# Gating matmuls behind the softmax normalisation in all four head quartets of an attention and FFN kernel, instead of the last one

## The chip, the cores and the metric

One Trainium2 chip with 8 NeuronCores. The batch of 32 sequences is split evenly, 4 sequences for each core, and every core runs the same program; there is no traffic between cores. The metric is the device time of one execution on the slowest core, in microseconds (us). TensorE is called PE here, ScalarE ACT, VectorE DVE, GpSimd POOL and SyncE SP.

## The reference

One pre-norm transformer layer on x of shape (32, 2048, 1024), in float32:

```
x = x + attention(layernorm(x))      # 16 heads of 64, additive mask, softmax over keys
x = x + ffn(layernorm(x))            # 1024 -> 64 -> (64x16 relu) -> 64 -> 1024

qkv    = encodings @ attn_w.T + attn_b
mask   = arange(n)[:, None] <= arange(n)[None, :]          # key <= query
scores = where(mask, einsum('bhki,bhqi->bhkq', k, q) / sqrt(64), -10000)
probs  = softmax(scores, axis=2)
out    = einsum('bhkq,bhkl->bhql', probs, v) -> @ out_w.T + out_b
```

## The kernel before

**Stages.** A core walks 16 stages: for each of its 4 sequences the four query blocks g = 0 to 3 of 512 queries. A stage is `attention(sq, g)`, then the output projection, second layernorm and FFN of its four 128-row tiles (`epilogueA`, `epilogueB`), interleaved with the layernorm, transposes and the Q, K and V projections of the next stage (`phaseA_ln`, `phaseA_tr`, `phaseA_qkv`).

**Order.** The program text is the order on each engine: each helper call appends one operation to the list of its engine, with the semaphore values that it must wait for. An engine runs its list in order; nothing passes a waiting instruction on the same engine. `deps` is what the operation waits for.

**Attention.** Query block g needs the key tiles kt = 0 to 4(g+1)-1 of 128 keys, so 4, 8, 12 or 16 of them. The 16 heads are handled as four quartets u = 0 to 3, each of two head pairs pi = 0 and 1. For each key tile and pair there are two score matmuls (L352, L356: the two heads of the pair, each contracting 64 rows in its own half of the array) into the 1024 float32 columns of P0 that belong to the pair, one exponential on ACT over both heads (L361) into `s_probs`, and, for the last four key tiles alone (the diagonal), a mask multiplication on DVE (L369). The value matmuls (L389, four for each key tile: two pairs by two heads) are emitted one key tile behind: scores of kt, then values of kt-1. They accumulate into P1 (pair 0) and P2 (pair 1); row 64 of each carries the softmax sum, because V has a column of ones.

**Normalisation.** Behind the last value matmul of a quartet, for each pair in turn: Ln of the sums (L404, on one partition by 1024), Exp of minus that (L407), a DMA of the 4 KB row to DRAM from ACT's queue (d1, L409), a DMA from POOL's queue that reads it back onto 64 partitions (d2, L411), and two DVE multiplications that write `s_comb` (L421) and so free the pair's P1 or P2. The first value matmuls of the next quartet wait for these multiplications (`pv_done`), since they overwrite the same banks. The scores of the next quartet wait for the exponentials that last read P0, and for nothing of the normalisation.

**The gating matmuls.** In the last quartet (u = 3) each pair's normalisation is followed on PE by three matmuls of 128x128 by 128 columns (L430), of the identity by itself, into columns 1536 to 1663 of P0. Nobody reads their result. The first waits for the pair's Ln, the second for its Exp, the third for the arrival of d2. Behind them on PE stands the output projection of `epilogueA`.

Of the kernel before, what the change touches and what calls it, by code (L numbers as in the profile page):

```python
# [95 lines left out]
def build_program(nseq=NSEQ):  # L96
# [20 lines left out]
    with ExitStack() as st:  # L117
# [11 lines left out]
        s_id = e(nc.sbuf_tensor("s_id", [128, 128], BF16))  # L129
# [14 lines left out]
        P0 = e(nc.psum_tensor("P0", [128, 2048], F32))  # L144
# [3 lines left out]
        s = Sched(nc)  # L148
# [181 lines left out]
        def attention(sq, g):  # L330
# [6 lines left out]
            for u in range(4):  # L337
# [3 lines left out]
                for kt in range(nkt + 1):  # L341
                    newpend = None
                    if kt < nkt:
# [4 lines left out]
                        for pi, hp in enumerate(pairs):  # L348
# [6 lines left out]
                                start=True, stop=True), deps=deps_sc)  # L355
# [3 lines left out]
                                start=True, stop=True), deps=[])  # L359
# [5 lines left out]
                                deps=[t_s1, st_["probs_pv"][pi * 2 + kt % 2]])  # L365
# [11 lines left out]
                    if pending is not None:  # L377
# [3 lines left out]
                        for pi, hp in enumerate(pairs):  # L381
                            for hi in range(2):
# [10 lines left out]
                                    start=f, stop=l, skip_group_check=True),  # L393
                                    deps=[pdeps[pi]] + dep_f)
                            st_["probs_pv"][pi * 2 + pkt % 2] = t_last_pv[pi]
                    pending = newpend
                for pi, hp in enumerate(pairs):
                    t_lp = t_last_pv[pi]
                    Ppv = P1 if pi == 0 else P2
                    zc = st_["zchain"] % 4  # L400
                    st_["zchain"] += 1
                    zrow = (s_zz[32:33, 0:1024] if pi == 0
                            else s_zz[96:97, 0:1024])
                    tln = s.op("act", lambda E, P=Ppv, zr=zrow: E.activation(  # L404
                        zr, P[64:65, 0:1024], AF.Ln),
                        deps=[t_lp, st_["zr_read"][pi], st_["zz_read"][pi]])
                    tex = s.op("act", lambda E, zr=zrow: E.activation(  # L407
                        zr, zr, AF.Exp, scale=-1.0), deps=[tln])
                    d1 = s.dma("act", f"ch_z{zc}", zscr.ap()[zc:zc + 1, :], zrow,  # L409
                               deps=[tex, st_["zscr_read"][zc]])  # L410
                    d2 = s.dma("pool", f"ch_zb{zc}", s_zz[pi * 64:(pi + 1) * 64, :],  # L411
                               bass.AP(zscr, zc * 1024, [[0, 64], [1, 1024]]),
                               deps=[d1, st_["zz_read"][pi]])
                    st_["zr_read"][pi] = d1
                    st_["zscr_read"][zc] = d2
                    for hi in range(2):
                        bank = 2 * pi + hi
                        hh = 2 * hp + hi
                        pvX = pv_banks[bank]
                        zb = s_zz[pi * 64:(pi + 1) * 64, hi * 512:(hi + 1) * 512]  # L420
                        tcm = s.op("dve", lambda E, P=pvX, c=hp, hh2=hh, z=zb: E.tensor_tensor(  # L421
                            s_comb[(hh2 % 2) * 64:(hh2 % 2) * 64 + 64, c * QB:(c + 1) * QB],
                            P[0:64, 0:512], z, ALU.mult),
                            deps=[d2, st_["comb_read"]])
                        st_["pv_done"][bank] = tcm
                        comb_written.append(tcm)
                    st_["zz_read"][pi] = comb_written[-1]
                    if u == 3:
                        for wdep in (tln, tex, d2):
                            s.op("pe", lambda E: E.matmul(  # L430
                                P0[:, 1536:1664], s_id[:, :], s_id[:, :],
                                start=True, stop=True), deps=[wdep])
            st_["P1_freed"] = comb_written[-1]
            st_["P2_freed"] = comb_written[-1]
            return comb_written
# [132 lines left out]
        phaseA_qkv(*stages[0])  # L568
        for idx, (sq, g) in enumerate(stages):
            comb = attention(sq, g)  # L570
            nxt = stages[idx + 1] if idx + 1 < len(stages) else None
            slot = lambda i: (idx * GT + i) % 6
# [109 lines left out]
```

How the kernel before makes its waits and increments, by code:

```python
            def run(engine):  # L80
                for emit, waits, inc_sem, inc in oplist:
                    for (sname, val) in waits:
                        engine.wait_ge(sems[sname], val)
                    ins = emit(engine)
                    if ins is not None and inc_sem is not None:
                        ins.then_inc(sems[inc_sem], inc)
```

## Time and profile before

| | us |
|---|---|
| time before, median of 2 runs (4315.42 to 4316.69) | 4316.06 |
| the profiled execution's own time | 4316.25 |
| its span, slowest core | 4314.3 |
| spans of the 8 cores | 4296.1 to 4314.3 |
| mean granted PE clock of the cores | 0.759 to 0.764 |
| PE busy | 2790.8 (65%) |
| PE weight loads busy | 1077.9 (25%) |
| ACT busy | 1803.0 (42%) |
| DVE busy | 1110.3 (26%) |

A busy share is an average over stages of different kinds. The granted clock is a share of full speed: 1.0 is 2.4 GHz and 0.5 is 1.2 GHz. In rows of the trace, "idle before" is the time that the engine stood still ahead of an instruction, with what released it; a row "x2" merges two instructions that follow each other.

### The profile page before, as it was taken

How to read it: one execution, taken by the hardware profiler on the slowest of the kernel's cores; microseconds unless marked ns; L12 is line 12 of the kernel's file. 1: busy time of each engine (PE TensorE's matmuls, PEld its weight loads, DVE VectorE, ACT ScalarE, POOL GpSimd, SP SyncE). 2: the span in 40 equal slices, each digit the busy share in tenths (PEclk: the TensorE clock that was granted, in tenths of full speed). 3: DMA queues.
4: the chain of work that ended last, by engine and by line, in shares of the span. 5: the costliest groups of instructions: out<-in, count | busy, mean ns of one | idle time of the engine just before them, and what ended most of it. 6: DMA issues, size and time to landing. Idle time of an engine off the chain costs nothing.

```text
span 4314.3 us, 40073 instructions; the slowest of 8 cores (4296.1 to 4314.3 us)
## 1 busy us (share of the span) xinstructions
PE 2790.8 (65%) x12384; PEld 1077.9 (25%) x12384; DVE 1110.3 (26%) x2486; ACT 1803.0 (42%) x2945; POOL 100.3 (2%) x196
## 2 busy tenths in 40 slices
PE   0657676686656658677674756757666576765874
PEld 0222232232222223232231312223222132322322
DVE  3141311402323141230323223031131413214112
ACT  0424337166141625517523251643733234272481
POOL 0000000000000000000000000000000000000000
PEclk9868787698676768768776776878877677776886
DMA  6010000100101000010000001000000000000000
GB/s 199 15 35 20 26 24 20 40 6 15 39 20 39 15 35 15 15 39 10 20 30 30 30 20 39 11 20 30 15 25 28 32 25 25 30 15 30 10 10 25
DMA packets 36934, 122.00 MB, mean 28 GB/s; under 512 B 7610, under 2 KB 7738, under 8 KB 36732
## 3 DMA queue, kind: packets, MB, share of 16 engines
q0 software_dynamic: 19456, 67.12, 4.4%
q1 hardware_dynamic: 17020, 51.80, 3.9%
q8 instruction: 110, 1.80, 0.2%
q14 instruction: 92, 0.75, 0.1%
q10 hardware_dynamic: 256, 0.52, 0.0%
HBM read 85.34 MB, written 34.08 MB: 28 GB/s over the span
## 4 chain that ended last, share of the span: by engine, by line
PE 48%; ACT 17%; DVE 11%; issue 11%; DMA 10%; ACTq 1%; DVEq 0%; SPq 0%; POOLq 0%
PE P L314 10%; PE P L389 10%; ACT s_probs L361 7%; PE P L291 6%; PE P L449 6%; DMA s_zz<-zscr 5%; PE P L352 5%; DMA zscr<-s_zz 3%; ACT s_zz L407 3%; ACT s_zz L404 3%; DVE s_xln L219 2%; DVE s_probs L492 2%; DVE s_x L460 2%; PE P L544 2%; PE P L548 2%
## 5 line engine op out<-in xcount | busy, mean ns | idle before, releaser
L361 ACT ACTIVATE s_probs<-P 128x1024 bf16<-128x1024 f32 (+3 forms) x1280 | 1062.8, 894 | 403.2 <-PE P L356 248.9
L389 PE MATMUL P<-s_probs,s_vaug 128*65 128x512 bf16 (+3 forms) x2560 | 721.7, 398 | 199.3 <-DVE s_comb L421 109.6
L352 PE MATMUL P<-s_q,s_k 64*128 64x512 bf16 (+3 forms) x1280 | 466.3, 392 | 429.4 <-ACT s_probs L361 395.0
L369 DVE TENSOR_TENSOR s_probs<-s_probs,s_tril 128x256 bf16<-128x256 bf16 x512 | 145.7, 292 | 1401.0 <-ACT s_probs L361 1398.6
L356 PE MATMUL P<-s_q,s_k 64*128 64x512 bf16 (+3 forms) x1280 | 475.3, 399 | 0.0
L314 PE MATMUL P<-s_xlnT,s_wqk 128*128 128x512 bf16 x2048 | 444.8, 379 | 0.0
L389 PEld LDWEIGHTS P<-s_probs,s_vaug 128*65 128x65 bf16 x2560 | 247.3, 119 | 568.1 <-issue 473.3
L449 PE MATMUL P<-s_ow,s_comb 128*128 128x512 bf16 x1024 | 331.4, 482 | 39.6 <-DVE s_x L552 39.6
L237 ACT ACTIVATE s_stats<-s_stats 128x1 f32<-128x1 f32 x128 | 37.7, 294 | 752.1 <-DVE s_stats L234 752.1
L421 DVE TENSOR_TENSOR s_comb<-P,s_zz 64x512 bf16<-64x512 f32 x256 | 175.0, 683 | 671.6 <-DMA s_zz<-zscr 667.6
L481 PE MATMUL P<-s_id,s_xln 128*128 128x128 bf16 x512 | 107.8, 258 | 370.4 <-ACT s_probs L488 276.2
L352 PEld LDWEIGHTS P<-s_q,s_k 64*128 64x128 bf16 x1280 | 108.9, 95 | 817.3 <-issue 811.4
L323 ACT ACTIVATE s_q<-P,s_bqk 128x512 bf16<-128x512 f32 x128 | 88.0, 688 | 449.8 <-PE P L314 449.8
L291 PE MATMUL P<-s_wv,s_xlnT 128*128 128x512 bf16 x1024 | 266.8, 408 | 8.3 <-ACT s_xlnT L276 8.3
L314 PEld LDWEIGHTS P<-s_xlnT,s_wqk 128*128 128x128 bf16 x2048 | 199.1, 98 | 241.5 <-issue 3.6
L276 ACT CAST s_xlnT<-P 128x128 bf16<-128x128 f32 x512 | 98.9, 274 | 181.8 <-PE P L270 181.0
L404 ACT ACTIVATE s_zz<-P 1x1024 f32<-1x1024 f32 x128 | 130.1, 1016 | 78.3 <-PE P L389 37.2
L449 PEld LDWEIGHTS P<-s_ow,s_comb 128*128 128x128 bf16 x1024 | 108.6, 115 | 216.6 <-issue 165.5
L219 DVE SCALAR_TENSOR_TENSOR s_xln<-s_x 128x1024 bf16<-128x1024 f32 x128 | 156.3, 1221 | 12.3 <-DMA s_x<-x 5.2
L481 PEld LDWEIGHTS P<-s_id,s_xln 128*128 128x128 bf16 x512 | 50.2, 105 | 425.2 <-issue 419.4
L300 DVE CAST s_vaug<-P 128x512 bf16<-128x512 f32 x128 | 88.8, 694 | 248.7 <-PE P L295 245.0
L270 PE MATMUL P<-s_id,s_xln 128*128 128x128 bf16 x512 | 76.8, 265 | 108.5 <-DVE s_xln L246 105.0
(60 smaller groups left out, 2028.4 us busy)
## 6 DMA issues: line engine op xcount, KB each, us to landing
s_x<-x SPq DMA_DIRECT2D x64, 512.0 KB, 4.0
s_zz<-zscr POOLq DMA_DIRECT2D x128, 256.0 KB, 3.5
out<-s_x POOLq DMA_DIRECT2D x64, 512.0 KB, 2.9
s_x<-wqk_t SPq DMA_DIRECT2D x16, 512.0 KB, 7.3
s_x<-wv_t SPq DMA_DIRECT2D x8, 512.0 KB, 6.2
s_x<-ow_t SPq DMA_DIRECT2D x8, 512.0 KB, 6.2
zscr<-s_zz ACTq DMA_DIRECT2D x128, 4.0 KB
s_x<-bias_rows SPq DMA_DIRECT2D x1, 260.0 KB
```

Source lines behind the costliest of these rows:

```text
L219: tsq = s.op("dve", lambda E: E.scalar_tensor_tensor(dst_xln[:, :], src[:, :], 1.0, src[:, :], ALU.mult, ALU.mult, accum_out=s_stats[:, cQ ...
L291: s.op("pe", lambda E, cc=c, ii=i, rr=r, p=pacc: E.matmul(p, s_xlnT[:, cc * QB + ii * 128: cc * QB + (ii + 1) * 128], s_wv[:, cc * 1024 + ...
L314: tmm = s.op("pe", lambda E, f=fc, cc=c, p=pacc: E.matmul(p, s_wqk[:, cc * 2048 + f * 128: cc * 2048 + (f + 1) * 128], s_xlnT[:, cc * QB:( ...
L352: s.op("pe", lambda E, c=hp, k=kt, c0=col0, S=SC: E.matmul(S[:, c0:512], s_k[0:64, c * T + k * 128: c * T + (k + 1) * 128], s_q[0:64, c * ...
L356: t_s1 = s.op("pe", lambda E, c=hp, k=kt, c0=col0, S=SC: E.matmul(S[:, 512 + c0:1024], s_k[64:128, c * T + k * 128: c * T + (k + 1) * 128] ...
L361: texp = s.op("act", lambda E, S=SC, pb=prb, c0=col0: E.activation(pb[:, :].rearrange("p (h c) -> p h c", h=2, c=512)[:, :, c0:512], S.rea ...
L369: dep_pv = s.op("dve", lambda E, pb=prb, c0=col0: E.tensor_tensor(pb[:, :].rearrange("p (h c) -> p h c", h=2, c=512)[:, :, c0:c0 + 128], p ...
L389: P=pv_banks[bank]: E.matmul(P[:, c0:512], s_vaug[:, ti * NH * 65 + hh2 * 65: ti * NH * 65 + hh2 * 65 + 65], pb[:, hi2 * 512 + c0: hi2 * 5 ...
L404: tln = s.op("act", lambda E, P=Ppv, zr=zrow: E.activation(zr, P[64:65, 0:1024], AF.Ln), deps=[t_lp, st_["zr_read"][pi], st_["zz_read"][pi]])
L421: tcm = s.op("dve", lambda E, P=pvX, c=hp, hh2=hh, z=zb: E.tensor_tensor(s_comb[(hh2 % 2) * 64:(hh2 % 2) * 64 + 64, c * QB:(c + 1) * QB], ...
L449: t_op = s.op("pe", lambda E, cc=c, rr=r, ii=i, P=PO: E.matmul(P[:, rr * 512:(rr + 1) * 512], s_comb[:, cc * QB + ii * 128: cc * QB + (ii ...
L481: ttr = s.op("pe", lambda E, a=xln, cc=c, v=tr_ap: E.matmul(v, a[:, cc * 128:(cc + 1) * 128], s_id[:, :], start=True, stop=True), deps=[tx ...
```

## The change

The condition `if u == 3:` is taken away. The three gating matmuls now follow the normalisation of both pairs in every quartet, so there are 24 of them in a stage instead of 6: 288 more on each core (16 stages x 3 quartets x 2 pairs x 3). In the quartets u = 0, 1 and 2, what stands behind them on PE is the first score matmul of the next quartet. Nothing else is changed.

```diff
                     st_["zz_read"][pi] = comb_written[-1]
-                    if u == 3:
-                        for wdep in (tln, tex, d2):
-                            s.op("pe", lambda E: E.matmul(
-                                P0[:, 1536:1664], s_id[:, :], s_id[:, :],
-                                start=True, stop=True), deps=[wdep])
+                    for wdep in (tln, tex, d2):
+                        s.op("pe", lambda E: E.matmul(
+                            P0[:, 1536:1664], s_id[:, :], s_id[:, :],
+                            start=True, stop=True), deps=[wdep])
             st_["P1_freed"] = comb_written[-1]
```

## Rows read from the trace of the kernel before

**Rows 1.** The page: chain that ended last, shares of the span by engine.

```profile
PE 48%; ACT 17%; DVE 11%; issue 11%; DMA 10%; ACTq 1%; DVEq 0%; SPq 0%; POOLq 0%
```

**Rows 2.** Waits of DVE ahead of L421, then of PE ahead of L430.

```profile
  DMA s_zz<-zscr: 667.6, 128
...
  DMA s_zz<-zscr: 135.9, 32
```

**Rows 3.** Timeline, boundary u = 0 to 1, g = 2: start us, us, engine, line, operation.

```profile
1693.95 1.02 ACT L404 ACTIVATE s_zz<-P 1x1024 f32<-1x1024 f32 x1 [0.66 <-PE P L389]
1694.03 0.39 PE L352 MATMUL P<-s_q,s_k 64*128 64x512 bf16 x1
...
1699.19 1.94 ACT L361 ACTIVATE s_probs<-P 128x1024 bf16<-128x1024 f32 x2 [0.43 <-ACT s_zz L407]
1700.36 0.58 PE L352 MATMUL P<-s_q,s_k 64*128 64x512 bf16 x1 [5.73 <-ACT s_probs L361]
...
1701.35 1.94 ACT L361 ACTIVATE s_probs<-P 128x1024 bf16<-128x1024 f32 x2 [0.22 <-issue]
...
1705.81 1.40 DVE L421 TENSOR_TENSOR s_comb<-P,s_zz 64x512 bf16<-64x512 f32 x2 [2.54 <-DMA s_zz<-zscr]
...
1706.64 1.32 PE L389 MATMUL P<-s_probs,s_vaug 128*65 128x512 bf16 x2 [2.61 <-DVE s_comb L421]
...
1707.90 0.60 PE L352 MATMUL P<-s_q,s_k 64*128 64x512 bf16 x1
...
1708.30 0.63 PE L352 MATMUL P<-s_q,s_k 64*128 64x512 bf16 x1
...
1708.63 1.94 ACT L361 ACTIVATE s_probs<-P 128x1024 bf16<-128x1024 f32 x2 [5.34 <-PE P L356]
1708.86 1.91 PE L389 MATMUL P<-s_probs,s_vaug 128*65 128x512 bf16 x4
...
1710.71 0.52 PE L352 MATMUL P<-s_q,s_k 64*128 64x512 bf16 x1
```

**Rows 4.** Windows, same boundary: PE, PEld, DVE, ACT, POOL busy (count), PEclk, DMA share, GB/s.

```profile
1698.00:1706.60 8.60, 2.43 (x6) 0.52 (x6) 2.12 (x4) 4.64 (x5) 1.05 (x2) 0.50 0.20 62
1706.60:1710.90 4.30, 4.15 (x12) 1.07 (x14) 0.61 (x1) 1.94 (x2) 0.00 (x0) 0.50 0.00 0
1711.10:1726.00 14.90, 12.92 (x68) 4.63 (x64) 1.52 (x6) 13.91 (x16) 0.00 (x0) 1.00 0.00 1
```

**Rows 5.** Timeline, the next boundary's first Ln.

```profile
1727.43 1.02 ACT L404 ACTIVATE s_zz<-P 1x1024 f32<-1x1024 f32 x1 [0.72 <-PE P L389]
```

**Rows 6.** Timeline, end of u = 3 of the stage before, with gating matmuls.

```profile
1516.67 1.02 ACT L404 ACTIVATE s_zz<-P 1x1024 f32<-1x1024 f32 x1 [0.53 <-DVE s_probs L369]
...
1524.90 0.52 PE L430 MATMUL P<-s_id 128*128 128x128 bf16 x3 [5.71 <-DMA s_zz<-zscr]
...
1528.41 1.40 DVE L421 TENSOR_TENSOR s_comb<-P,s_zz 64x512 bf16<-64x512 f32 x2 [2.15 <-DMA s_zz<-zscr]
...
1528.45 0.27 PE L430 MATMUL P<-s_id 128*128 128x128 bf16 x1 [3.03 <-DMA s_zz<-zscr]
...
1528.58 1.87 PE L449 MATMUL P<-s_ow,s_comb 128*128 128x512 bf16 x4
```

**Rows 7.** Windows, same end of u = 3.

```profile
1524.80:1532.00 7.20, 4.07 (x12) 1.47 (x12) 4.90 (x7) 0.00 (x0) 0.51 (x1) 0.50 0.10 36
```

**Rows 8.** Timeline, first key tiles of u = 0, g = 2.

```profile
1670.41 0.37 PE L352 MATMUL P<-s_q,s_k 64*128 64x512 bf16 x1 [1.04 <-ACT s_k L323]
...
1675.06 0.60 PE L352 MATMUL P<-s_q,s_k 64*128 64x512 bf16 x1
```

**Rows 9.** Timeline, g = 0: u = 0 from its first score, then boundary u = 0 to 1.

```profile
157.75 0.37 PE L352 MATMUL P<-s_q,s_k 64*128 64x512 bf16 x1 [1.03 <-ACT s_k L323]
...
165.43 1.02 ACT L404 ACTIVATE s_zz<-P 1x1024 f32<-1x1024 f32 x1 [0.64 <-PE P L389]
...
176.83 1.40 DVE L421 TENSOR_TENSOR s_comb<-P,s_zz 64x512 bf16<-64x512 f32 x2 [2.18 <-DMA s_zz<-zscr]
178.26 0.90 DVE L369 TENSOR_TENSOR s_probs<-s_probs,s_tril 128x256 bf16<-128x256 bf16 x4
178.70 1.89 PE L389 MATMUL P<-s_probs,s_vaug 128*65 128x512 bf16 x4 [5.37 <-DVE s_probs L369]
180.52 0.39 PE L352 MATMUL P<-s_q,s_k 64*128 64x256 bf16 x1
...
183.95 1.02 ACT L404 ACTIVATE s_zz<-P 1x1024 f32<-1x1024 f32 x1 [0.74 <-PE P L389]
```

## The prediction

> **What bounds the kernel now.** I read the page's chain first, to see whether the work around the edit is on it at all. The chain holds 10% DMA and 17% ACT beside 48% PE [rows 1], although the transfers are tiny: a latency stands on the path. Next the waits by line. All 128 pairs' multiplications (L421) wait for the DMA that brings the reciprocal sums back, 667.6 us together, and the gating matmuls that exist already (u = 3) wait 135.9 us for the same DMA, 32 times [rows 2]. Each of the 64 quartets ends in such a round trip. Then the timeline of one boundary between quartets, and the granted clock of its parts, show what PE and ACT do during it.
>
> Call the boundary's key tiles by the next quartet's kt: S0 is its first score matmuls, V0 its first value matmuls, "landing" the arrival of pair 1's d2, which is where the second pair of L421 begins. In [rows 3] Ln of pair 0 starts at 1693.95 and S0 of the next quartet at 1694.03, beside it. ACT does Ln and Exp of both pairs, and from 1699.19 to 1703.29 four exponentials, those of key tiles 0 and 1 for both pairs (two rows of x2). S1 goes out at 1700.36. The landing is at 1705.81. V0 of pair 1 starts at 1706.64 and S2 at 1707.90, so 2.09 after the landing. So before the landing two of the quartet's key tiles have had their scores and exponentials. That run-ahead is what the reader is to see: 4 x 0.97 = 3.88 us of ACT work hidden in the round trip.
>
> Is it worth anything later? Yes: from 1711.10 to 1726.00 ACT is busy 13.91 of 14.9 us and the clock is full [rows 4]. Within the quartet ACT is the bound, with about 7% slack; exponentials pushed out of the gap aren't made up for.
>
> **The change, part by part.**
>
> *The matmuls themselves.* 288 more of 128 columns. The existing ones take 0.27 alone, and the work behind the last one starts 0.13 after it (1528.45, 1528.58), itself 0.04 behind the landing (1528.41) [rows 6]. Only the last of six is on the path: 0.17 us for each of the 48 boundaries, 8 us, counted below. The other five lie in PE's idle time.
>
> *The waits.* Two of the six hold PE until Ln or Exp is done, and the last until the landing. Behind them on PE stands S0, with S1 and V0 behind it; ACT's first exponentials wait for S0. What moved work costs is therefore the chain from the landing to S2. With an unmasked start (g = 1, 2, 3), after the landing: 0.17 to S0; 0.73 from a score pair to its exponential (1707.90 to 1708.63); two exponentials of 0.97 in sequence, because S1 of pair 1 has to wait until its half of P0 is read; 0.20 from there to S1 of pair 1 (1700.16, the end of the first exponential, to 1700.36); 0.56 to V0 (1708.30 to 1708.86, low clock); 1.85 from V0 to S2 (1708.86 to 1710.71) [rows 3]. Sum 0.17 + 0.73 + 1.94 + 0.20 + 0.56 + 1.85 = 5.45 us. It was 2.09. At S2 both kernels have the same work done, so the quartet is 3.36 us late.
>
> *The clock.* In [rows 4] the clock stays at 0.50 while PE is busy 2.43 of 8.6 us, and is 1.00 from about 1711, behind 4.3 us in which PE was busy 4.15. Before the change the key tile from S2 to S3 runs at low clock and takes 2.81 us (1707.90 to 1710.71); at full clock the exponentials bound it at 1.94. So one tile is worth 0.87. If the rise stays where it is against the landing (5.2 us behind it), the changed kernel has that tile at full clock and gets 0.87 back: 2.5 us. If the rise moves along with the value matmuls, which now start about 3 us later, nothing comes back: 3.36. If it comes one tile later still: 4.2.
>
> *A bound from below.* Quartet u = 0 already starts in the manner that the change gives to the others, from S0 with nothing run ahead. From its S0 (1670.41) [rows 8] to its Ln (1693.95) [rows 3] are 23.54 us; with 0.17 ahead that makes 23.71. Quartet u = 1 takes from its landing (1705.81) [rows 3] to its Ln (1727.43) [rows 5] 21.62. The difference is 2.09 us. Since u = 0 starts at full clock (S0 takes 0.37 there, and its S0 to S2 takes 4.65 [rows 8] against 5.28 in my sum) it is a low end. I take 3.0 for these boundaries, between 2.5 and 3.36 and nearer the second, because PE has little to do between S0 and V0 and the rise followed dense work. Bounds 2.1 and 4.2.
>
> *g = 0.* Here all four key tiles are masked, and DVE works in order: the masks of the next quartet stand behind the multiplications that wait for the landing (multiplications 176.83, masks 178.26, V0 178.70). So part of the run-ahead was worthless already: S2 comes 3.69 behind the landing (180.52) [rows 9]. After the change the same chain as above with 1.82 at its end (178.70 to 180.52) makes 5.42, the masks lying beside it, so 1.73 late. The u = 0 comparison gives 157.75 to 165.43, 7.68 + 0.17, against 176.83 to 183.95, 7.12 [rows 9]: 0.73 late, again from a full-clock start. I take 1.5; bounds 0.7 and 2.3 (1.73 and two thirds of a low-clock tile).
>
> *What costs nothing.* The DMAs are not touched, their issue on ACT and POOL neither. Ln to landing takes 11.74 where the gating matmuls are there already (1516.67 to 1528.41) [rows 6] and 11.86 where they aren't (1693.95 to 1705.81) [rows 3], so they neither delay nor speed the round trip. The matmuls' write into P0 waits for Ln, which stands behind the last exponential on ACT: no new wait. The 16 ends of u = 3 stay as they are.
>
> *Sum.* 36 boundaries (12 stages of g = 1 to 3, three each) x 3.0 = 108, and 12 (g = 0) x 1.5 = 18: 126 us. Against the profiled execution's own 4316.25 us (span 4314.3 and 1.95 around it; 0.2 over the runs' median of 4316.06) that gives 4442 us, 2.9% slower. Low ends: 36 x 2.1 + 12 x 0.7 = 84, so 4400. With 3.36 and 1.73: 142, so 4458.
>
> **The rivals.**
>
> *The matmuls keep the clock up.* They break an idle stretch of 5.73 [rows 3] on PE. If full clock were held through the boundary, S0 to S2 would take 4.65 [rows 8], 4.82 with the 0.17, so 2.73 late, and the tile behind it would give 0.87 back: 1.9. In g = 0 some 0.4. Sum 36 x 1.9 + 12 x 0.4 = 73, 4389 us, 1.7%: within 2%. This is the case on the other side of my forecast. Against it: where these matmuls stand now, the stretch from 1524.80 to 1532.00 has clock 0.50 all the same [rows 7], with idle times of 5.71 and 3.03 between them [rows 6]. Chance 0.09.
>
> Beside that row, the Trainium skill, "TensorE: Matmul & The Clock Gate", section "Loop structure matters more than you think", shows as its bad pattern a long DMA wait placed between bursts of matmuls, which sends PE to its lower clock, and as the good one work that follows at once. By that rule the change, which puts PE's next matmuls behind a DMA, is no way to hold the clock; the trace agrees for u = 3 (0.50). It would speak for my sum and against the rival just told.
>
> *The low clock lasts longer.* PE now does almost nothing before the landing, where it did 2.43 of 8.6 us [rows 4], and then a sparse start. If the rise comes one tile later than S3: 36 x 4.2 + 12 x 2.3 = 179, 4495 us. For it: u = 0 falls even from full clock to 0.60 us matmuls at 1675.06 after its sparse start [rows 8]. Chance 0.08.
>
> *The delay is made up.* Were ACT not the bound, a late start would be caught up inside the quartet, and only the 8 us of gating matmuls would be left: 4324 us. The 7% of ACT idle [rows 4] would allow it about 1 us in 15. The u = 0 comparison, a whole quartet long, has 2.09 left at its end. Chance 0.05.
>
> *Faster.* That would need the landing to move forward by more than 3 us in each boundary; the 11.74 against 11.86 speaks against it. Chance 0.03.
>
> **How the numbers follow.** The forecast, slower by 84 to 142 us, has 0.75. A measurement of this kernel can tell about 2% from no change, that is 86 us, 4402. Slower by over 2%: 0.75 less its low edge, and the low-clock case: 0.80. Within 2%: the held clock, the made-up delay and the low edge: 0.17. Faster: 0.03. The range of 8 in 10 goes from 4385, which takes in the held clock, to 4475, half way into the long-low-clock case.
>
> **What would show each step.** In the profile after: 384 matmuls at the gating line, 128 of them waiting for s_zz<-zscr; S0 0.17 behind the landing and no L361 between the second Exp (L407) and the landing; S2 about 5.4 behind it; landing to Ln of about 24.6 at g = 2 (21.62 now) and 8.6 at g = 0 (7.12 now); ACT busy unchanged at 1803; the granted clock 0.50 through the landing. It would be wrong if the clock were 1.0 at the landing, if Ln to landing left 11.7, or if landing to Ln grew by under 2 us.

## The result, and the profile after

The changed kernel is slower: 1.0297 times the time before, with a 95% interval of 1.0256 to 1.0338. Beside a median of 4318.42 us for the kernel before in the same runs that is about 4447 us, where 4442 was predicted. A few runs of both kernels in which one die was slow are left out of the ratio.

The page after, its head and the engines' shares of the chain (share of the span), against [rows 1]:

```profile
span 4453.8 us, 40841 instructions; the slowest of 8 cores (4420.9 to 4453.8 us)
...
PE 2835.7 (64%) x12672; PEld 1106.2 (25%) x12672; DVE 1113.1 (25%) x2486; ACT 1801.5 (40%) x2945; POOL 100.3 (2%) x196
...
PE 48%; ACT 19%; issue 11%; DVE 10%; DMA 10%; ACTq 1%; DVEq 0%; SPq 0%; POOLq 0%
```

ACT does the same work as before (1801.5 against 1803.0 us), but its share of the chain went from 17% to 19%: work that lay beside the round trip now lies on the path. The slowest core of this execution, core 5, also started late: its first Ln is at 178.1 us, on core 7 of the kernel before at 165.4. That part of the 4453.8 has nothing to do with the change. From first to last Ln it needs 4170.6 us (178.1 to 4348.7) where core 7 before needed 4043.7 (165.4 to 4209.1):

```profile
L404 ACT ACTIVATE s_zz<-P x128: 1015/1016/1017, 178.1 to 4348.7; 1x1024 f32<-1x1024 f32 x128
```

The difference is 126.9 us. Of the eight cores, each beside the same core before, it is 111 to 127.

Who PE waited for at the gating line (idle us, times), the row that answers to [rows 2]:

```profile
L429 PE MATMUL P<-s_id 128*128 128x128 bf16 x384 | 79.1, 252 | 668.6 <-DMA s_zz<-zscr 544.1
```

384 matmuls, and 544.1 us of waiting for the DMA instead of 135.9, in 128 waits instead of 32. On the other hand no value matmul waits for the multiplications L421 any more; before they did so 71 times, 109.6 us together. The timeline of the boundary u = 0 to 1 at g = 2, the same place as [rows 3]:

```profile
1761.71 1.02 ACT L404 ACTIVATE s_zz<-P 1x1024 f32<-1x1024 f32 x1 [0.67 <-PE P L389]
...
1773.33 1.40 DVE L421 TENSOR_TENSOR s_comb<-P,s_zz 64x512 bf16<-64x512 f32 x2 [2.72 <-DMA s_zz<-zscr]
1773.37 0.26 PE L429 MATMUL P<-s_id 128*128 128x128 bf16 x1 [3.59 <-DMA s_zz<-zscr]
1773.57 0.60 PE L352 MATMUL P<-s_q,s_k 64*128 64x512 bf16 x1
...
1774.30 1.02 ACT L361 ACTIVATE s_probs<-P 128x1024 bf16<-128x1024 f32 x1 [7.78 <-PE P L356]
...
1775.47 0.58 PE L352 MATMUL P<-s_q,s_k 64*128 64x512 bf16 x1 [0.87 <-ACT s_probs L361]
...
1776.38 0.58 PE L352 MATMUL P<-s_q,s_k 64*128 64x512 bf16 x1 [0.31 <-ACT s_probs L361]
...
1776.92 1.92 PE L389 MATMUL P<-s_probs,s_vaug 128*65 128x512 bf16 x4
...
1778.77 0.39 PE L352 MATMUL P<-s_q,s_k 64*128 64x512 bf16 x1
```

ACT stands still for 7.78 us ahead of its first exponential; in [rows 3] it had done four by then. S2 is at 1778.77, 5.44 behind the landing at 1773.33; it was 2.09. The windows, against [rows 4] (PE, PEld, DVE, ACT, POOL busy, then the granted clock):

```profile
1765.00:1773.40 8.40, 0.55 (x4) 0.37 (x4) 1.44 (x3) 1.43 (x2) 1.05 (x2) 0.51 0.21 63
1773.40:1776.90 3.50, 2.33 (x9) 0.45 (x9) 1.29 (x2) 2.38 (x3) 0.00 (x0) 0.50 0.00 0
1776.90:1780.20 3.30, 3.30 (x14) 1.02 (x12) 0.00 (x0) 2.41 (x3) 0.00 (x0) 0.72 0.01 2
1782.00:1796.00 14.00, 12.15 (x64) 4.40 (x62) 1.51 (x6) 13.19 (x17) 0.00 (x0) 1.00 0.00 1
```

PE is busy 0.55 of 8.4 us ahead of the landing, at clock 0.51. The gating matmuls don't hold it up.

Over all boundaries of the slowest core: mean time from the landing (the start of pair 1's L421) to the next quartet's first Ln (L404), 12 boundaries for each g, in us. The last column is twelve times the sum of the differences to the kernel before, over g. For the changed kernel, each of the eight cores beside the same core before, it is 118 to 124 us. The experiments below stand here too.

| kernel | g = 0 | g = 1 | g = 2 | g = 3 | 48 boundaries, against before |
|---|---|---|---|---|---|
| before | 7.39 | 14.00 | 21.68 | 29.53 | |
| changed | 9.09 | 16.64 | 24.57 | 32.50 | +122 |
| wait alone, no matmuls | 8.85 | 16.28 | 24.33 | 32.54 | +113 |
| gates for Ln and Exp alone | 7.48 | 14.00 | 21.81 | 29.47 | +2 |
| matmuls alone, no new wait | 7.49 | 13.93 | 22.11 | 29.53 | +5 |
| gate for pair 0 alone | 7.46 | 13.50 | 21.97 | 29.62 | -1 |
| wait at S1 instead of S0 | 7.47 | 13.98 | 22.27 | 29.55 | +8 |
| changed, and 48 dense matmuls | 7.82 | 15.90 | 24.10 | 31.10 | +76 |
| distance two | 6.56 | 12.30 | 20.15 | 27.94 | -68 |
| distance two, not in quartet 0 | 6.58 | 12.39 | 20.10 | 27.99 | -66 |

The way from the first Ln to the landing is the same in all of them, 11.4 to 11.7 us in the mean of a g.

### The profile page after: what moved, and what is told of

Read it like the earlier page. It is cut to its first block, busy times and chain, and to the rows that moved or that the text cites. A ratio compares the mean times of both kernels' runs of the same rounds, so it can differ in the third digit from the quotient of the medians.

```text
span 4453.8 us, 40841 instructions; the slowest of 8 cores (4420.9 to 4453.8 us)
## 1 busy us (share of the span) xinstructions
PE 2835.7 (64%) x12672; PEld 1106.2 (25%) x12672; DVE 1113.1 (25%) x2486; ACT 1801.5 (40%) x2945; POOL 100.3 (2%) x196
## 4 chain that ended last, share of the span: by engine, by line
PE 48%; ACT 19%; issue 11%; DVE 10%; DMA 10%; ACTq 1%; DVEq 0%; SPq 0%; POOLq 0%
PE P L314 10%; PE P L389 10%; ACT s_probs L361 9%; PE P L291 6%; PE P L352 6%; PE P L448 6%; DMA s_zz<-zscr 5%; DMA zscr<-s_zz 3%; ACT s_zz L407 3%; ACT s_zz L404 3%; DVE s_xln L219 2%; DVE s_probs L491 2%; DVE s_x L459 2%; PE P L543 2%; PE P L547 2%
## 5 line engine op out<-in xcount | busy, mean ns | idle before, releaser
L389 PE MATMUL P<-s_probs,s_vaug 128*65 128x512 bf16 (+3 forms) x2560 | 684.4, 391 | 16.7 <-DVE s_probs L369 14.8
L352 PE MATMUL P<-s_q,s_k 64*128 64x512 bf16 (+3 forms) x1280 | 478.5, 400 | 200.3 <-ACT s_probs L361 163.6
L429 PE MATMUL P<-s_id 128*128 128x128 bf16 x384 | 79.1, 252 | 668.6 <-DMA s_zz<-zscr 544.1
L356 PE MATMUL P<-s_q,s_k 64*128 64x512 bf16 (+3 forms) x1280 | 488.0, 407 | 0.0
L314 PE MATMUL P<-s_xlnT,s_wqk 128*128 128x512 bf16 x2048 | 453.8, 384 | 0.0
L480 PE MATMUL P<-s_id,s_xln 128*128 128x128 bf16 x512 | 106.9, 257 | 370.9 <-ACT s_probs L487 276.4
L421 DVE TENSOR_TENSOR s_comb<-P,s_zz 64x512 bf16<-64x512 f32 x256 | 174.8, 683 | 669.7 <-DMA s_zz<-zscr 665.7
L429 PEld LDWEIGHTS P<-s_id 128*128 128x128 bf16 x384 | 38.9, 101 | 707.2 <-issue 704.1
L404 ACT ACTIVATE s_zz<-P 1x1024 f32<-1x1024 f32 x128 | 130.1, 1016 | 78.1 <-PE P L389 37.9
```

The source lines that it names most:

```text
L314: tmm = s.op("pe", lambda E, f=fc, cc=c, p=pacc: E.matmul(p, s_wqk[:, cc * 2048 + f * 128: cc * 2048 + (f + 1) * 128], s_xlnT[:, cc * QB:( ...
L352: s.op("pe", lambda E, c=hp, k=kt, c0=col0, S=SC: E.matmul(S[:, c0:512], s_k[0:64, c * T + k * 128: c * T + (k + 1) * 128], s_q[0:64, c * ...
L356: t_s1 = s.op("pe", lambda E, c=hp, k=kt, c0=col0, S=SC: E.matmul(S[:, 512 + c0:1024], s_k[64:128, c * T + k * 128: c * T + (k + 1) * 128] ...
L389: P=pv_banks[bank]: E.matmul(P[:, c0:512], s_vaug[:, ti * NH * 65 + hh2 * 65: ti * NH * 65 + hh2 * 65 + 65], pb[:, hi2 * 512 + c0: hi2 * 5 ...
L404: tln = s.op("act", lambda E, P=Ppv, zr=zrow: E.activation(zr, P[64:65, 0:1024], AF.Ln), deps=[t_lp, st_["zr_read"][pi], st_["zz_read"][pi]])
L480: ttr = s.op("pe", lambda E, a=xln, cc=c, v=tr_ap: E.matmul(v, a[:, cc * 128:(cc + 1) * 128], s_id[:, :], start=True, stop=True), deps=[tx ...
```

## The experiments

The theory: the loss is the run-ahead of two key tiles that no longer lies in the round trip, and it is the wait for pair 1's DMA alone that takes it away. The rivals: the added matmuls cost by themselves; any wait costs, wherever it ends; the loss is one of clock.

**The wait without the matmuls.** The next quartet's S0 waits for the landing, and no matmul is added. `d2s` holds the d2 of both pairs of the quartet that has just ended.

```diff
+                            if u > 0 and kt == 0:
+                                deps_sc = deps_sc + d2s
...
+                d2s = []
...
+                    d2s.append(d2)
```

> The kernel before, in which the first scores of each quartet but the first wait for the arrival of the last quartet's reciprocal sums, without any new matmul. Theory (the wait costs, through the run-ahead that it takes away): S0 about 0.1 us behind the landing, landing to the next Ln about 2.8 us longer than before for g = 1 to 3 and 1.6 longer for g = 0, so 2.5 to 2.9% slower than before, 5 to 15 us faster than the changed kernel, whose six matmuls cost 0.24 us at 48 boundaries. Rival (the added matmuls themselves cost): within 0.5% of the kernel before.

Measured: 1.0259 (1.0234 to 1.0284), from two executions. The whole loss but a tenth comes without a single added matmul. S0 stands 0.04 behind the landing and not 0.24, as in the changed kernel; the table's difference between the two is 10 us, 0.2 for each of 48 boundaries:

```profile
956.91 1.40 DVE L425 TENSOR_TENSOR s_comb<-P,s_zz 64x512 bf16<-64x512 f32 x2 [2.25 <-DMA s_zz<-zscr]
956.95 0.58 PE L354 MATMUL P<-s_q,s_k 64*128 64x512 bf16 x1 [11.07 <-DMA s_zz<-zscr]
```

**The matmuls without the wait.**

```diff
-                    for wdep in (tln, tex, d2):
+                    for wdep in ((tln, tex, d2) if u == 3
+                                 else (st_["last_exp"][1],) * 3):
```

> The changed kernel in which the six gating matmuls of quartets 0, 1 and 2 wait for the quartet's last exponential alone, which the next scores wait for in any case. All 288 matmuls are there, no wait is new. Theory: the next scores go out 0.5 to 0.7 us later into a PE idle time of 5.7 us, nothing else moves: within 0.2% of the kernel before. Rival (the matmuls cost by themselves, or hold the clock up and gain): outside of 0.5%.

Measured: 1.0009 (0.9994 to 1.0024). The six matmuls take 0.49 us ahead of S0 (timeline, g = 3), the four exponentials of the run-ahead start where they did, and nothing is late:

```profile
952.28 0.49 PE L430 MATMUL P<-s_id 128*128 128x128 bf16 x6
...
957.52 3.82 ACT L361 ACTIVATE s_probs<-P 128x1024 bf16<-128x1024 f32 x4 [0.43 <-ACT s_zz L407]
```

**Gates that end earlier.** First the ones for Ln and Exp alone, then all three of pair 0 alone.

```diff
+                    for wdep in ((tln, tex, d2) if u == 3 else (tln, tex)):
```

> The changed kernel with the third gating matmul, the one that waits for the DMA, left out of quartets 0, 1 and 2; the ones for Ln and Exp stay (192 new matmuls). Theory (only a wait that lasts beyond the end of ACT's normalisation costs): the first scores go out 4.8 us behind the first Ln, ACT is free for them only then anyway, so the four exponentials of the run-ahead start 0.7 to 0.9 us later and still end before the landing; S2 stays 2.1 us behind the landing: within 0.3% of the kernel before (4300 to 4330 us). Rival (any gating costs, by the number of matmuls or by their waits): two thirds of the change's loss, about 2% slower.

Measured: 1.0013 (0.998 to 1.0046).

```diff
+                    for wdep in ((tln, tex, d2) if u == 3 or pi == 0 else ()):
```

> The changed kernel with the three gating matmuls of quartets 0, 1 and 2 behind pair 0's normalisation alone (144 new matmuls, the last waits for pair 0's DMA). Pair 0's data land 7.7 us behind the first Ln, pair 1's 11.6 behind it. Theory (the loss is the length of the chain from the gate to S2, where it is not hidden by the round trip): S0 at 7.9 behind Ln, S2 5.3 later at 13.2 to 13.4, where the kernel before has 13.7: no loss for g = 1 to 3, the four exponentials ending about 1 us later than the landing of pair 1 at most; within 0.5% of the kernel before, and more than 2% faster than the changed kernel. Rival (a wait for a DMA costs its idle time wherever it is): half of the change's loss or more, 1.4%.

Measured: 0.9982 (0.9938 to 1.0026). This one waits for a DMA too and costs nothing. In its timeline (g = 3; first Ln at 958.73) pair 0's gate opens at 966.32, S0 goes out at 966.52, the four exponentials run from 967.26 to 971.08, past the landing at 970.21, and S2 is at 972.29, 2.08 behind the landing, as in the kernel before (2.09):

```profile
958.73 1.02 ACT L404 ACTIVATE s_zz<-P 1x1024 f32<-1x1024 f32 x1 [0.71 <-PE P L389]
...
966.32 0.27 PE L429 MATMUL P<-s_id 128*128 128x128 bf16 x1 [5.06 <-DMA s_zz<-zscr]
...
966.52 0.60 PE L352 MATMUL P<-s_q,s_k 64*128 64x512 bf16 x1
...
967.26 3.82 ACT L361 ACTIVATE s_probs<-P 128x1024 bf16<-128x1024 f32 x4 [3.71 <-PE P L356]
...
970.21 1.40 DVE L421 TENSOR_TENSOR s_comb<-P,s_zz 64x512 bf16<-64x512 f32 x2 [2.52 <-DMA s_zz<-zscr]
...
972.29 0.60 PE L352 MATMUL P<-s_q,s_k 64*128 64x512 bf16 x1
```

S0 may thus be held back until 7.8 us behind the first Ln (966.52 less 958.73) for nothing, and the next 3.9 us, to pair 1's landing, cost 2.6 to 3.0 at g = 1 to 3. The kernel before had slack in this chain; the change used it up with pair 0's gate and paid for pair 1's.

The table's row is that of core 1. On cores 4 to 7 the 48 boundaries are even 11 to 17 us shorter than on the same cores before, and the clock rises there 3.1 to 5.1 us behind the landing in the mean of a g = 1 to 3, where it rose 5.1 to 6.3 behind it. With S0 held back, S1 and pair 0's V0 stand right ahead of the landing, so PE's work lies closer together. That this is the reason is not shown, and the ratio can't tell such a gain from none.

**No gating matmuls at all.** The six at the end of quartet 3 are taken out of the kernel before.

> The kernel before without its six gating matmuls at the end of quartet 3. Theory: what stands behind them there, the output projection, waits for the multiplications that follow the same landing, so a wait for the landing costs nothing there: within 0.2% of the kernel before. The clock at the end of quartet 3 falls in the same place with and without them. Rival (the gating matmuls keep the clock higher and earn something there): slower by 0.3% or more.

Measured: 1.001 (0.9969 to 1.005). The form that the change copies has no effect that can be told in its own place: there, the work behind it waits for the same landing in any case.

**Half of the run-ahead.** S0 goes out early, S1 waits for the landing.

```diff
+                            if u > 0 and kt == 1:
+                                deps_sc = deps_sc + d2s
...
+                d2s = []
...
+                    d2s.append(d2)
```

> The kernel before, in which the scores of the second key tile (S1) of quartets 1 to 3 wait for the landing, those of the first (S0) do not: half of the run-ahead is taken away, no matmul is added. Theory: behind the landing come S1 of both pairs at once (P0 is free by then), V0, and S2 at about 2.8 us where it was 2.1, and the exponentials of S1 start 0.8 behind the landing: 0.7 to 1.2 us for each of 48 boundaries, so 0.8 to 1.3% slower than before. That is less than half of the change's loss, because the first key tile's scores and exponentials start the chain and the second only lengthen it. Rival (each tile of run-ahead is worth the same): 1.4 to 1.5% slower.

Measured: 1.0037 (0.9993 to 1.0082), a miss: at most the lower end of what was expected, and in the profile 8 us instead of 34 to 58. The chain itself came out as worked out, S2 at 2.86 behind the landing instead of 2.09. But most of the 0.77 us was given back by the clock. The windows, first of this kernel behind the landing at 2004.03 (g = 3), then of the kernel before behind its own at 1991.56:

```profile
2004.00:2007.00 3.00, 2.93 (x10) 0.92 (x12) 1.37 (x2) 1.94 (x2) 0.00 (x0) 0.50 0.00 0
2007.60:2030.00 22.40, 19.15 (x91) 6.67 (x91) 0.86 (x3) 21.73 (x24) 0.00 (x0) 1.00 0.00 0
```

```profile
1991.60:1994.60 3.00, 2.10 (x6) 0.39 (x6) 1.33 (x2) 0.22 (x1) 0.00 (x0) 0.50 0.00 0
1994.60:1997.10 2.50, 2.50 (x10) 0.67 (x8) 0.00 (x0) 1.72 (x2) 0.00 (x0) 0.50 0.00 0
1998.00:2019.00 21.00, 18.35 (x90) 6.52 (x89) 1.17 (x4) 20.27 (x24) 0.00 (x0) 1.00 0.00 0
```

S1 now follows the landing at once and V0 follows S1 without a gap, so PE is busy 2.93 of the first 3 us instead of 2.10, and the clock is full from 3.6 behind the landing on, where before it was still 0.50 at 5.5 behind it. In the trace's record of the granted clock, over 12 boundaries each, the rise lies 4.2, 5.6 and 4.1 us behind the landing at g = 1, 2 and 3 (before: 6.3, 5.6 and 5.6). It is g = 2, where it did not come earlier, that shows the chain's delay in the table: 22.27 against 21.68. The other cores bear this out, each beside the same core before, at g = 2: where the rise comes 1.3 to 1.6 us earlier (cores 2, 4 and 6), a boundary is 0.1 to 0.2 us longer, and where it comes 0.4 earlier (cores 0 and 1), 0.5.

**The clock held up.** 48 matmuls of 512 columns ahead of the gates, added to the changed kernel.

```diff
+                if u < 3:
+                    for _ in range(48):
+                        s.op("pe", lambda E: E.matmul(
+                            P0[:, 1536:2048], s_id[:, :], s_wv[:, 0:512],
+                            start=True, stop=True), deps=[st_["last_exp"][1]])
```

> The changed kernel with 48 matmuls of 512 columns, with a result that nobody reads, put ahead of the gating matmuls in quartets 0, 1 and 2; at full clock they fill about 10.3 of the 11.6 us from Ln to landing. It measures what the clock is worth at the boundary. Theory: the clock stays 1.0 through these boundaries, S0 to S2 takes 4.7 to 4.8 us where it takes about 5.3, the key tile behind S2 takes 1.95 to 2.0 where it takes 2.8: 1.1 to 1.4 us less for each boundary of g = 1 to 3, about 1 us less for g = 0, so about 50 to 60 us less than the changed kernel, and still 1.3 to 1.7% slower than before, because the run-ahead stays lost. Rival (the loss of the change is a loss of clock): back to the time of the kernel before. Rival (the clock falls all the same, or the dense matmuls cost power): no faster than the changed kernel.

Measured: 1.0162 (1.0081 to 1.0243), from two executions, so about 1.3% faster than the changed kernel and still slower than before; 47 us less by the table (core 5), 52 to 61 on the other cores. In size it is what was expected, but not in its course. The windows of one boundary at g = 2:

```profile
1727.70:1738.10 10.40, 10.40 (x52) 4.74 (x51) 1.37 (x2) 4.03 (x4) 1.05 (x2) 1.00 0.15 51
1739.30:1742.40 3.10, 1.58 (x9) 0.37 (x8) 1.23 (x2) 2.45 (x3) 0.00 (x0) 0.81 0.00 0
1743.00:1749.00 6.00, 6.00 (x20) 1.46 (x18) 0.00 (x0) 3.88 (x5) 0.00 (x0) 0.58 0.00 0
```

The clock is 1.00 up to the landing. Behind it S1 waits for exponentials, PE is busy 1.58 of 3.1 us, and the clock falls just then, to come back only some microseconds later. It does so in 34 of this core's 48 boundaries: in 10 of 12 at g = 2, which gained 0.5 us a boundary, and in 6 of 12 at g = 3, which gained 1.4. On core 4, where it falls in 3 of 12 at g = 2, that g gained 1.4 as well. So the sparse restart often throws away a clock that was held up with 10 us of dummy work.

**More run-ahead.** The value matmuls two key tiles behind the scores; six buffers for the exponentials.

```diff
+        s_probs = s_probs + [s_xln[2], s_xln[3]]
...
-                for kt in range(nkt + 1):
+                pendq = []
+                for kt in range(nkt + 2):
...
-                            prb = s_probs[pi * 2 + kt % 2]
+                            prb = s_probs[pi * 3 + kt % 3]
...
-                    if pending is not None:
-                        pkt, pcol0, pdeps, pprobs = pending
+                    if kt >= 2:
+                        pkt, pcol0, pdeps, pprobs = pendq.pop(0)
...
+                    if newpend is not None:
+                        pendq.append(newpend)
```

> The other direction: the kernel before with the value matmuls two key tiles behind the scores instead of one, and six buffers for the exponentials instead of four (the two added ones are the layernorm buffers of the epilogue, idle during attention). At a boundary three key tiles of scores and exponentials run ahead of the landing instead of two. Theory (run-ahead in the round trip is what counts, and ACT is the bound behind it): two more exponentials, 1.94 us, move into the idle stretch of each of the 36 boundaries of g = 1 to 3, some of it lost to the low clock; less or nothing for g = 0, whose masks wait behind the multiplications: 1.0 to 1.9 us x 36, so 0.8 to 1.6% faster than before. Rival (the round trip and the low clock behind it set the boundary, not ACT): within 0.3% of the kernel before.

Measured: 0.987 (0.9821 to 0.992), faster. The distance and the number of buffers were changed together; more buffers alone were not run. Two more exponentials start ahead of the landing at 1693.97 (g = 2; the two added buffers are called s_xln):

```profile
1691.81 1.02 ACT L362 ACTIVATE s_probs<-P 128x1024 bf16<-128x1024 f32 x1
1692.73 1.02 ACT L362 ACTIVATE s_xln<-P 128x1024 bf16<-128x1024 f32 x1
1693.97 1.40 DVE L423 TENSOR_TENSOR s_comb<-P,s_zz 64x512 bf16<-64x512 f32 x2 [2.28 <-DMA s_zz<-zscr]
```

Each boundary of g = 1 to 3 is 1.5 to 1.7 us shorter, for 1.94 us of ACT work moved. The 48 boundaries give 68 us; the span gave 44 (4270.2 against 4314.3). In quartet 0, which has no round trip ahead of it, the time from its first score to its Ln grew, at g = 3 from 31.08 to 32.43 in the mean of four. So distance two was then kept to quartets 1 to 3.

```diff
+                lag = 1 if u == 0 else 2
+                for kt in range(nkt + lag):
...
+                    if kt >= lag:
```

> The kernel with value matmuls two key tiles behind the scores, but in quartets 1 to 3 alone; quartet 0, which has no round trip ahead of it, keeps its distance of one. In the profile of the kernel with distance two everywhere, landing to Ln was shorter by 0.8 us (g = 0) and 1.5 to 1.7 us (g = 1 to 3), 68 us in 48 boundaries, while quartet 0 was longer by 0.8 to 1.4 us from its first score to its Ln, about 17 us in 16 stages. Theory (running ahead pays only where there is a round trip to hide it in): the 17 us come back, 4250 to 4262 us, 1.3 to 1.6% faster than before. Rival (quartet 0's length is given by the quartet's form whatever its distance, or the gain was noise): no change against distance two everywhere, 4270 us.

Measured: 0.9847 (0.9721 to 0.9972). The interval is wide, but the profile tells the two apart: span 4243.7 against 4270.2 us, the gain at the boundaries unchanged (66 us), quartet 0 at g = 3 back at 31.35. Its profiled execution is the shortest of the study.

**Holding the clock where dense work follows.** The same 48 matmuls, in the kernel before, at the end of quartet 3.

> The kernel before with 48 matmuls of 512 columns, with a result that nobody reads, ahead of the gating matmuls at the end of quartet 3, where the output projection follows. Theory: unlike the gating matmuls they hold the clock at 1.0 up to the landing, and the projection, which is dense, goes on at it: its first eight matmuls take 1.9 us instead of 3.4 to 3.6 and the next eight 1.9 instead of 2.2 to 2.5: 1.6 to 2.2 us at each of 16 ends, 25 to 35 us, 0.6 to 0.8% faster. Rival (the clock at the projection isn't on the path, or falls right behind the landing as it did in the quartets' sparse starts): within 0.2%.

Measured: 0.9967 (0.9918 to 1.0016), no change that can be told. The clock did what was expected, the time did not. This kernel's end of a quartet 3, landing at 1531.46, first the window behind the landing, with a granted clock of 1.00, then the timeline:

```profile
1531.50:1536.00 4.50, 4.36 (x18) 1.66 (x19) 4.12 (x8) 0.00 (x0) 0.00 (x0) 1.00 0.00 0
```

```profile
1531.84 1.67 PE L454 MATMUL P<-s_ow,s_comb 128*128 128x512 bf16 x7
...
1533.76 1.90 PE L454 MATMUL P<-s_ow,s_comb 128*128 128x512 bf16 x8
...
1537.10 0.81 DVE L246 TENSOR_SCALAR s_xln<-s_x,s_stats 128x1024 bf16<-128x1024 f32 x1
...
1538.06 0.59 PE L270 MATMUL P<-s_id,s_xln 128*128 128x128 bf16 x4 [2.08 <-DVE s_xln L246]
...
1538.44 3.23 PE L454 MATMUL P<-s_ow,s_comb 128*128 128x512 bf16 x8
```

The projection runs at full clock (one of its first eight matmuls has no record), and then PE waits 2.08 us for a layernorm on DVE. That layernorm starts behind L421 and ends its chain with L246 5.64 us behind the landing. In the kernel before, L246 is just as far behind:

```profile
1528.58 3.57 PE L449 MATMUL P<-s_ow,s_comb 128*128 128x512 bf16 x8
...
1534.05 0.81 DVE L246 TENSOR_SCALAR s_xln<-s_x,s_stats 128x1024 bf16<-128x1024 f32 x1
...
1535.43 1.89 PE L449 MATMUL P<-s_ow,s_comb 128*128 128x512 bf16 x8
```

(1534.05 less the 1528.41 of [rows 6]). At the low clock the projection was just about as long as DVE's work beside it. The faster clock turned 2 us of matmuls into 2 us of waiting. And behind that wait it was lost again: the next eight matmuls of the projection took 3.23 us, where the kernel before took 1.89 (1535.43). Over the whole span PE stood still 136.9 us ahead of L270 for L246, in 19 waits, where it was 105.0 us in 9.

**Both together.**

> Both of the two changes just told, distance two in quartets 1 to 3 and 48 dense matmuls at the end of quartet 3. Theory: they touch different boundaries and add up: 4220 to 4235 us, 1.9 to 2.3% faster than before. Rival (the chip gives the clock back elsewhere, or the cores of a die slow each other down at the higher load): less than the better of the two alone.

Measured: 0.9843 (0.9721 to 0.9964), from two executions, beside 0.9847 for distance two in quartets 1 to 3 alone. The interval is too wide to tell the 0.6 to 0.8% that the dense matmuls were expected to add. The two executions took 4252 and 4266 us, neither in the 4220 to 4235 that were expected, and in the profile cores 0 to 3 end at 4235.8 to 4252.4 us, where they ended at 4222.5 to 4242.9 with distance two alone. So no gain of the dense matmuls is to be seen, as the run before would have it: the second term of the expected sum failed.

## Why the prediction was right

**The sum.** Predicted were 126 us; the two profiles have 126.9 us more from first to last Ln on their slowest cores, and the table has 122 us in the 48 boundaries. For g = 1 to 3 the steps said 3.0 for each, measured 2.64, 2.89 and 2.97. For g = 0 they said 1.5, measured 1.70. The 3.0 and the 1.5 were choices inside of bounds; the one came out somewhat high (0.36 at g = 1) and the other low, so that a small part of the agreement is two errors against each other.

**The chain from the landing to S2.** Predicted 5.45, measured 5.47, 5.47 and 5.45 in the means of g = 1 to 3, and 5.34 at g = 0 (predicted 5.42). Its terms were off by little and against each other. S0 comes 0.24 behind the landing, not 0.17: from the last gating matmul to it are 0.20 (1773.37 to 1773.57), against 0.13 ahead of the output projection [rows 6]. From S0 to S1 of pair 1 are 2.81 instead of 2.87 (1773.57 to 1776.38), and from there to V0 0.54 instead of 0.56 (1776.38 to 1776.92).

**That ACT cannot make it up** is shown by the wait alone: there S2 is 3.2 us later behind the landing than before (5.25 and 2.09 in the mean of g = 1), and at the quartet's end 2.3, 2.7 and 3.0 us of it are left.

**The clock.** I took 3.0 between 2.5 (the rise stays where it is against the landing) and 3.36 (it moves along with the value matmuls). It moved by part of the way: in the record of the granted clock it lies 6.6 to 7.7 us behind the landing in the mean of a g, where it lay 5.6 to 6.3. The gains and losses follow it. In the boundary shown above the rise comes early, 5.5 behind the landing; S2 already takes 0.39 there, and the next Ln follows 23.92 behind the landing. In the four boundaries of g = 2 in which it comes 8.4 to 8.6 behind, that is 24.92 to 25.03. The low-clock rival, one tile more, did not come.

**The held-clock rival** fell: 0.51 ahead of the landing. What the run with 48 dense matmuls adds is that it would have been a loss even so, 76 us by the table (60 to 71 on the other cores), against the 73 that I had worked out for it. But this is partly luck. I had left the clock full behind S0, and it is not.

**That the gating matmuls cost 8 us** was right in size (10 between the table's rows), and that the 240 others lie in idle time as well (5 us in the table for all 288, with the interval on 1.0).

**What the prediction did not see.** It gave the whole loss to the landing without asking how late S0 may be before it costs anything. The answer, from pair 0's gate, is at least 7.8 us behind the first Ln. A later one that is still free was not looked for; an estimate is 8.4, from the landing at 11.5, S2 at 2.09 behind it and the 5.23 from S0 to S2 (5.47 less 0.24). With that the change could have been read as two: the gates for both Ln, both Exp and pair 0's DMA, which the two runs with them show to be free, and the one for pair 1's DMA, which brings the loss. And the half-way experiment showed that the price isn't the length of the chain alone: a chain 0.77 longer but without a gap was nearly free, where the clock rose earlier.

## What to carry to other kernels

Before a wait is put on an engine's in-order queue, look at what stands behind it there: here it was the next quartet's scores, through them four exponentials of the engine that bounds the quartet, and those had filled the round trip. Slack is to be measured as the latest start that still meets the event behind the stall, not as idle time; up to that point waiting is free, and the work to move into the stall is that of the engine that bounds what follows. The Trainium skill's "TensorE: Matmul & The Clock Gate", section "Why this matters for your kernels", asks for no long idle gaps on PE. The runs agree that dense work holds the clock (1.00 for 10 us), but what that is worth depends on what follows: ahead of the quartets it gave back 47 of 122 us, at the end of quartet 3, where a layernorm on DVE set the pace, nothing that could be told.

## What the runs showed of the hardware that was not expected

Six matmuls of 128 columns spread over 11.6 us left the clock at 0.50 at the landing, 48 of 512 columns kept it at 1.00. With the clock at 1.00, a stretch in which PE was busy 1.58 of 3.1 us was followed by 0.58 over the next 6 us, in which it was busy throughout. At the end of a quartet 3, with the clock at 1.00, a wait of 2.08 us was followed by eight matmuls that took 3.23 us instead of 1.89. And a start without a gap brought the rise to 3.6 us behind the landing in one boundary, where a start with a gap had it later than 5.5; in the means it was 4.2 and 4.1 instead of 6.3 and 5.6 at g = 1 and 3, and 5.6 in both at g = 2.
